# Edge messages of a graph network on one core: the gathered rows are added to the edge products in PSUM, and the gates stay in PSUM

## The reference, cut to what matters

```
edge_input = concatenate([x[src], edge_attr])                  # 200000 x (96 + 32)
messages = gelu(edge_input @ mW1 + mb1) @ mW2 + mb2
gates = sigmoid(gelu(edge_input @ gW1 + gb1) @ gW2 + gb2)      # one number for each edge
aggregated = segment_sum(messages * gates, dst)
```

## Time and profile before

| what | value |
|---|---|
| median of 3 executions | 5472.3 us (5466.99 to 5479.78) |
| the profiled execution's own time | 5465.93 us |
| span in its profile | 5464.0 us |
| busy: PE, DVE, ACT, POOL | 3652.2, 3789.0, 2527.0, 3536.7 us |
| gathers of line 790 for `rows` | 1568, 1791.1 us busy |
| they start between | 1519.8 and 3842.4 us |

### The profile page before, as it was taken

One profiled execution on the slowest core, in us unless ns is written; L12 is line 12 of the kernel. 1 busy time (PEld: TensorE's weight loads), 2 busy tenths in 40 slices (PEclk: granted clock), 3 DMA queues, 4 the chain that ended last, 5 costly groups with the idle time before them and its releaser, 6 DMA issues.

```text
span 5464.0 us, 92238 instructions
## 1 busy us (share of the span) xinstructions
PE 3652.2 (67%) x33772; PEld 2286.6 (42%) x33772; DVE 3789.0 (69%) x5678; ACT 2527.0 (46%) x4379; POOL 3536.7 (65%) x2920
## 2 busy tenths in 40 slices
PE   4899899999953333333333333333279999999999
PEld 3888899899931111111111111111233333333333
DVE  7999432544455665665665655655379999999999
ACT  5999110101023233233333233332158888888887
POOL 3699100000057777777777777777448888888888
PEclk9999999999966666666666666666589999999999
DMA  3344889698733333333333333333111212222121
GB/s 70 165 200 191 331 340 394 256 398 336 292 90 115 117 114 115 118 110 117 117 110 119 117 111 117 117 111 118 46 35 57 64 57 60 60 58 64 57 63 38
DMA packets 296561, 760.10 MB, mean 139 GB/s; under 512 B 81161, under 2 KB 183753, under 8 KB 289993
## 3 DMA queue, kind: packets, MB, share of 16 engines
q1 hardware_dynamic: 217496, 595.47, 29.4%
q0 software_dynamic: 78768, 160.85, 11.2%
HBM read 589.77 MB, written 166.38 MB: 138 GB/s over the span
## 4 chain that ended last, share of the span: by engine, by line
PE 41%; POOL 34%; issue 15%; DVE 6%; ACT 1%; another core or an unknown queue 1%; DVEq 1%; DMA 0%; ACTq 0%; POOLq 0%; SPq 0%
POOL GA L790 32%; PE p_e L1167 14%; PE p_tr L1307 10%; PE p_e L1292 9%; PE p_mm L1269 3%; PE p_mm L1098 1%; POOL VA L790 1%; DVE VA L2423 1%; PE p_tr L1026 1%; DVE VA L1965 1%; POOL VA L902 1%; PE p_tr L1085 1%; DVE VA L1963 1%; PE p_e L1244 0%
## 5 line engine op out<-in xcount | busy, mean ns | idle before, releaser
L790 POOL DMA_INDIRECT GA<-table_mg,VA x1568 | 1791.1, 1142 | 1487.9 <-DMA table_mg<-VA 955.4
L2423 DVE TENSOR_TENSOR VA<-VA,p_mm 128x1024 f32<-128x1024 f32 (+1 forms) x1204 | 1362.0, 1203 | 7.5 <-POOL VA L902 6.6
L902 POOL TENSOR_SCALAR VA<-VA 128x1024 f32<-128x1024 f32 (+1 forms) x1204 | 1236.2, 1046 | 168.8 <-ACT VA L1644 157.0
L1198 PE MATMUL p_e<-BD,EA 128*128 128x384 f32 x784 | 407.1, 671 | 731.9 <-DMA EA<-in_edge_t 731.3
L1644 ACT ACTIVATE VA<-p_e 128x1024 f32<-128x1024 f32 x602 | 615.8, 1023 | 178.6 <-PE p_e L1292 177.5
L1307 PE MATMUL p_tr<-VA,GA 128*32 128x512 f32 (+1 forms) x5096 | 641.8, 580 | 2.7 <-ACT GA L1664 2.1
L2235 DVE TENSOR_TENSOR GA<-GA 128x1344 f32<-128x1344 f32 x168 | 254.2, 1554 | 542.7 <-DMA GA<-table_mg,VA 530.1
L2263 DVE SCALAR_TENSOR_TENSOR R<-R,keep,M 128x97 f32<-128x97 f32 x1568 | 505.8, 323 | 124.8 <-issue 8.2
L1198 PEld LDWEIGHTS p_e<-BD,EA 128*128 128x128 f32 x784 | 205.0, 270 | 916.9 <-DMA EA<-in_edge_t 765.1
L1198 PE MATMUL p_tr<-BD,EA 128*128 128x384 f32 x392 | 210.8, 669 | 370.9 <-DMA EA<-in_edge_t 370.9
L1198 PE MATMUL p_mm<-BD,EA 128*128 128x384 f32 x392 | 207.4, 660 | 374.0 <-DMA EA<-in_edge_t 374.0
(11 more groups left out here) (267 smaller groups left out, 6616.6 us busy)
## 6 DMA issues: line engine op xcount, KB each, us to landing
GA<-adj SPq DMA_DIRECT2D x98, 800.0 KB, 6.1
VA<-adj SPq DMA_DIRECT2D x98, 800.0 KB, 6.1
run_m<-R SPq DMA_DIRECT2D x112, 700.0 KB, 3.9
GA<-adj SPq DMA_DIRECT2D x98, 768.0 KB, 6.1
VA<-adj SPq DMA_DIRECT2D x98, 768.0 KB, 6.1
H<-adj SPq DMA_DIRECT2D x56, 896.0 KB, 5.1
adj<-GA SPq DMA_DIRECT2D x25, 1568.0 KB, 5.3
adj<-VA SPq DMA_DIRECT2D x24, 1568.0 KB, 5.3
```

The source lines that it names most:

```text
L790: pool.indirect_dma_start(out=to, out_offset=None, in_=of, in_offset=bass.IndirectOffsetOnAxis(ap=at, axis=0)).then_inc(s, 16)
L902: pool.tensor_scalar(e, e, HIGH, LOW, ALU.min, ALU.max).then_inc(clipped, 1)
L1198: pe.matmul(p_h[m % len(p_h)][0:CH, 0:4 * D], EA[:, n % 2, k // 2, :], BD[:, 2 * (k % 2):2 * (k % 2) + 2, :, :].rearrange("p a b f -> p (a ...
L2423: dve.tensor_tensor(e, e, p_mm[n % 2][:, 0:cols_of(n)].unsqueeze(1).to_broadcast([P, 2, cols_of(n)]), ALU.mult).then_inc(weighed, 1)
```

## The change

ScalarE no longer copies the edge products to SBUF. VectorE reads them in PSUM as one input of the addition, takes the gathered rows as the other, and writes to `hid` in SBUF. The 28 halves of 96 columns of a batch are packed five to a PSUM bank (480 columns), so that a batch has 6 packs (`PACKS`) in place of 7 banks. A pack that crosses the border of a group of `EA` (768 columns) is made by two matmuls. `p_h` has seven banks; the eighth, `p_mm[1]`, holds `gate_row` (copied there once) and `gates`, which ScalarE's tanh now writes there. `hid` has two slots in place of four. TensorE waits on `rows_added`, since it is VectorE that frees a bank now.

```diff
-AHEAD_E = 2
-SLOTS_E = 4
+SLOTS_E = 2
+PACK = 5
+PACKS = -(-2 * U // PACK)
+ADDS = PACKS
...
-        p_h = [*p_e, *p_tr, *p_mm]
+        p_h = [*p_e, *p_tr, p_mm[0]]
...
-        gate_row = gw2[0:CH, :]
-        gates = small[:, 1, 0:U]
+        gate_row = p_mm[1][0:CH, 0:D]
+        gates = p_mm[1][0:CH, D:D + U]
...
+        def pack_halves(b):
+
+            return range(PACK * b, min(PACK * b + PACK, 2 * U))
...
                     if k >= 2:
-                        sp.wait_ge(edge_product, BANKS * (k - 1))
+                        sp.wait_ge(edge_product, PACKS * (k - 1))
...
-                    wait(pool, rows_added, 2 * (k - 1))
+                    wait(pool, rows_added, ADDS * (k - 1))
...
-                for m in range(BANKS * BATCHES):
-                    n, k = m // BANKS, m % BANKS
-                    if k == 0:
+                for m in range(PACKS * BATCHES):
+                    n, b = m // PACKS, m % PACKS
+                    if b == 0:
                         pe.wait_ge(edge_landed[n % 2], 16 * (n // 2 + 1))
-                    wait(pe, edges_kept, m - len(p_h) + 1)
-                    pe.matmul(p_h[m % len(p_h)][0:CH, 0:4 * D], EA[:, n % 2, k // 2, :],
-                              BD[:, 2 * (k % 2):2 * (k % 2) + 2, :, :].rearrange("p a b f -> p (a b f)"),
-                              start=True, stop=True).then_inc(edge_product, 1)
+                    wait(pe, rows_added, m - len(p_h) + 1)
+                    at_col = 0
+                    for g in range(UG):
+                        part = [v for v in pack_halves(b) if v // (2 * EG) == g]
+                        if not part:
+                            continue
+                        cols = slice(D * (part[0] - 2 * EG * g), D * (part[-1] + 1 - 2 * EG * g))
+                        mm = pe.matmul(p_h[m % len(p_h)][0:CH, at_col:at_col + D * len(part)], EA[:, n % 2, g, :],
+                                       BD[:, :, :, :].rearrange("p a b f -> p (a b f)")[:, cols], start=True, stop=True)
+                        at_col += D * len(part)
+                    mm.then_inc(edge_product, 1)
...
-                def keep_edges(n):
-
-                    wait(act, sums_ready[n % 2], (n - SLOTS_E) // 2 + 1)
-                    for k in range(BANKS):
-                        m = BANKS * n + k
-                        act.wait_ge(edge_product, m + 1)
-                        act.activation(hid[n % SLOTS_E][:, 2 * k:2 * k + 2, :],
-                                       p_h[m % len(p_h)][0:CH, 0:4 * D].rearrange("p (a f) -> p a f", a=2), ACT.Copy
-                                       ).then_inc(edges_kept, 1)
...
+                dve.tensor_copy(gate_row, gw2[0:CH, :])
...
-                    dve.wait_ge(edges_kept, BANKS * (n + 1))
                     dve.wait_ge(rows_landed[n % 2], 16 * U * (n // 2 + 1))
-                    for c in (0, 1):
-                        half = hid[n % SLOTS_E][:, BANKS * c:BANKS * (c + 1), :]
-                        dve.tensor_tensor(half, half, rows[:, n % 2, BANKS * c:BANKS * (c + 1), :], ALU.add
+                    of = rows[:, n % 2, :, :].rearrange("p u f -> p (u f)")
+                    for b in range(PACKS):
+                        m = PACKS * n + b
+                        dve.wait_ge(edge_product, m + 1)
+                        dve.tensor_tensor(hid_at[n % SLOTS_E][:, pack_cols(b)],
+                                          p_h[m % len(p_h)][0:CH, 0:D * len(pack_halves(b))], of[:, pack_cols(b)], ALU.add
                                           ).then_inc(rows_added, 1)
```

More of the change, by code:

```diff
@@ L346, in build @@
         p_sums = p_tr[0]
-        gate_row = gw2[0:CH, :]
-        gates = small[:, 1, 0:U]
+        gate_row = p_mm[1][0:CH, 0:D]
+        gates = p_mm[1][0:CH, D:D + U]
         rows = GA[0:CH, 0:2 * U * 2 * D].rearrange("p (h u f) -> p h u f", h=2, u=U)
-        hid_at = [*[GA[0:CH, (2 + k) * U * 2 * D:(3 + k) * U * 2 * D] for k in range(SLOTS_E - 1)], VA[0:CH, 0:U * 2 * D]]
+        hid_at = [GA[0:CH, (2 + k) * U * 2 * D:(3 + k) * U * 2 * D] for k in range(SLOTS_E)]
         hid = [a.rearrange("p (u f) -> p u f", u=U) for a in hid_at]
-        assert (SLOTS_E + 1) * U * 2 * D <= GA.shape[1] and U * 2 * D <= TILES * D
+        assert (SLOTS_E + 2) * U * 2 * D <= GA.shape[1]
         half_bias = small[:, 2, 0:1]
@@ L525, in products, with pack_cols @@
             return sum(len(bank_tiles(g, n_w)) for g in range(groups))
+        def pack_halves(b):
+            return range(PACK * b, min(PACK * b + PACK, 2 * U))
+        def pack_cols(b):
+            return slice(D * pack_halves(b).start, D * pack_halves(b).stop)
         def acc_steps(a):
@@ L1191, in sum_pass @@
                 pe.wait_ge(product_used, at["mm"])
[L1193 to L1195 removed]
+                for m in range(PACKS * BATCHES):
+                    n, b = m // PACKS, m % PACKS
+                    if b == 0:
                         pe.wait_ge(edge_landed[n % 2], 16 * (n // 2 + 1))
[L1197 to L1201 removed]
+                    wait(pe, rows_added, m - len(p_h) + 1)
[9 more added lines that the diff above has]
+                    mm.then_inc(edge_product, 1)
+                pe.wait_ge(rows_added, PACKS * BATCHES)
                 update_nodes()
@@ L1572, in sum_pass @@
             def sum_pass():
-                def keep_edges(n):
-                    wait(act, sums_ready[n % 2], (n - SLOTS_E) // 2 + 1)
-                    for k in range(BANKS):
-                        m = BANKS * n + k
-                        act.wait_ge(edge_product, m + 1)
-                        act.activation(hid[n % SLOTS_E][:, 2 * k:2 * k + 2, :],
-                                       p_h[m % len(p_h)][0:CH, 0:4 * D].rearrange("p (a f) -> p a f", a=2), ACT.Copy
-                                       ).then_inc(edges_kept, 1)
-                act.wait_ge(table_stored, 16 * GROUPS * 2)
-                for n in range(AHEAD_E):
-                    keep_edges(n)
                 for n in range(BATCHES):
-                    for c in (0, 1):
-                        half = hid[n % SLOTS_E][:, BANKS * c:BANKS * (c + 1), :]
-                        act.wait_ge(rows_added, 2 * n + c + 1)
-                        act.activation(half, half, ACT.Gelu).then_inc(gelu_done, 1)
+                    for lo, hi in ((0, PACKS // 2), (PACKS // 2, PACKS)):
+                        some = hid_at[n % SLOTS_E][:, pack_cols(lo).start:pack_cols(hi - 1).stop]
+                        act.wait_ge(rows_added, PACKS * n + hi)
+                        act.activation(some, some, ACT.Gelu).then_inc(gelu_done, 1)
                     act.wait_ge(logit_ready, n + 1)
                     act.activation(gates, small[:, 0, 0:U], ACT.Tanh, bias=half_bias, scale=0.5).then_inc(gate_ready, 1)
-                    if n + AHEAD_E < BATCHES:
-                        keep_edges(n + AHEAD_E)
             def scatter_pass(n):
```

4 lines of the change are left out of this document (removed).

## The result

Three runs of the changed kernel took 5420.28 to 5426.13 us, median 5422.25, against 5472.3 before: a ratio of 0.9905, 95% interval 0.9889 to 0.992. So it is faster, but by 50 us, under 1%, and not by 331, and lies outside the range (5122 to 5185). The profiled execution took 5426.13 us with a span of 5424.2.

What follows compares the result with a forecast made beforehand. GpSimd's issue of 1568 gathers was taken as the bound; 332 us of port holds gained less 1 us lost gave 5472.3 - 331 = 5141 us, with an 8-in-10 range of 5122 to 5185 us.

Steps and rivals of the forecast that it cites:

- Point 1: VectorE's additions and two multiplications lose one SBUF input and stop holding GpSimd's gathers: 332 us gained.
- Rivals A and B: A: port not freed in all three places, 5240 to 5260, both 5360 us (7%); B: nothing gained, 5472 us (4%).
- Point 2: VectorE's turn per batch grows by 0.3 to 14.2 us, still waiting some 3.3 us within 17.5 us of gathers.
- Point 4: TensorE's nine matmuls a batch take some 10 us, covered with 7.5 us to spare; uncovered, up to 10 us per batch.
- rival C: Slower: products come late at TensorE's waits on `rows_added`, turns of 24.2 us, 414 us more, 5890 us (2%).
- Rival D: Transfers cannot follow the gathers' faster pace: loss of perhaps 20 to 50 us, 5160 to 5190 us (3%).
- Point 5: Gathers wait for `rows_added` of batch k - 2: no wait but the first, once (29.8 us, some 0.5 more).
- the sum itself: Gather stage: 1567 steps of 0.949 + 0.302 us make 1960 us, with 29.8 us of waiting 1990, against 2322.6.
- the 29.8 us of the sum: GpSimd's one wait at the start of the gather stage, counted in the 1990 us.
- The holds: Long VectorE instructions with two SBUF inputs lengthen gathers beside them: mean 1142 ns against median 949, 303 us busy time.
- the gather's 0.94 us beside the addition: Sign for point 1: the gather at 3899.56 keeps its usual 0.94 us amid a 0.56 us addition from PSUM.
- the "odd 33 us" of point 1: Idle time of the gathers beyond 470 us, read as some 17 late starts at 1.91 us each, some rounding included.

Runs made afterwards that it cites:

- the third chip: Chip of the third follow-up group: kernel before 5406.1 us; changed kernel with one memset per gather 5099.58, two memsets 5100.19, a drain behind each 14 gathers 5368.63.
- groups one, two, four and five: Follow-up groups, each on another chip; the kernel before took 5474.7 us (first), 5480.3 (second), 5475.4 (fourth) and 5473.7 (fifth).

## Why the prediction was wrong

**What was right.** Point 1, the port: additions and multiplications with one input in PSUM don't hold gathers, in any of the three places and in either order of inputs (maximum 1046 ns). This is what the Trainium skill, page "SBUF — State Buffer", section "Who interferes with whom", says of VectorE instructions with at most one SBUF input, and the trace agrees. Rivals A and B are out. Point 2, VectorE's own work in a turn: 14.2 us forecast, 14.07 measured with the gathers left out. (1344 columns in 1.5 us are 0.90 columns per ns, and not the 0.96 of point 2 unless a fixed part is taken off first. The six additions took the 3.3 us all the same, from 2985.42 to 2988.69.) Point 4: with the gathers left out TensorE keeps up with turns of 14.07 us, and in the changed kernel no addition waited for a product that was still being made, so rival C is out. Rival D is out as well: the additions waited 2.1 us for rows in the whole stage. Point 5 held only where there are no stalls; in the changed kernel gathers waited 286.6 us for rows to be freed. And the sum itself came out on the third chip: the gathers start within 1993.2 us, where I had 1990:

```profile
L798 POOL DMA_INDIRECT GA<-table_mg,VA x1568: 940/946/4881, 1521.9 to 3515.1; - x196
...
L2240 DVE TENSOR_TENSOR GA<-p_e,GA x384: 446/648/659, 1554.1 to 3518.8; 128x480 f32<-128x480 f32 x160, 128x288 f32<-128x288 f32 x32
...
  DMA GA<-table_mg,VA: 389.7, 111
```

These are the rows of the kernel with one memset ahead of each gather, whose turn is the changed kernel's in all but that. VectorE's additions wait there for rows alone, 389.7 us in 111 turns or 3.5 us in each, where I had written "some 3.3 us"; they never wait for TensorE. The ratio was 0.9426, against a forecast of 5141 / 5472.3 = 0.9395. The changed kernel itself was not run on such a chip, so that it would take the same there is not shown.

**The step that failed.** Point 2 says "a batch of 14 gathers at 1.25 us will take 17.5 us, so VectorE still waits some 3.3 us in each turn", and rival D "gathers between the held ones already go at that pace". Both take for granted that the pace of one engine leaves the others' work as long as it was: that VectorE's turn stays 14.2 us beside gathers at 1.25 us, and that it is VectorE that waits. Measured were turns of 19.96 us, with GpSimd waiting for VectorE. On five of seven occasions (the first result and the chips of groups one, two, four and five) gathers that come at 1.25 us for longer than some 21 in a row make instructions of VectorE come late, and of ScalarE too, above all where it has copies to make (run sums mostly 1.40 us apart, at times 0.72, in place of 0.39), until GpSimd pauses. TensorE was not late. Gathers between the held ones go at 1.25 us, but never many of them.

The size. The stage was to last 1990 us and lasted 2264.4. Of the 274 us between them, 257 are what GpSimd waited for VectorE beyond the 29.8 us of the sum (286.6 in all); the rest are late starts. The holds had been (1142 - 949) ns x 14 = 2.7 us a batch, the drain that clears the stalls costs 2.7, and GpSimd's waiting is 2.56 a batch, so all three come out at 20 to 20.4 us. Why they lie so near to each other no run shows; it may be chance. It is not that the gathers' mean pace decides: with one wait for six products they were 1.48 us apart on average and with `gate_row` and `gates` alone 1.50, more than the 1.46 of the kernel before, and the stalls stayed. What the kernel before has instead is breaks: the holds themselves, and only 11 of its run sums come late. With `gate_row` and `gates` alone some 0.7 us of them are left in a batch, (998 - 949) ns x 14, and there are stalls. So I read the holds as no mere loss: on such a chip they did for the others what the drain does. The changed stage took 58.2 us less (2264.4 for 2322.6), began 12.6 us later, and what comes behind it took 5.8 us more: 39.8 us of span.

That taking away the two multiplications' holds alone was slower (ratio 1.0132) fits the same cause: less pause, and ScalarE's seven copies a batch left as work for the stalls to fall on. The full change takes those copies away, and this may be why it gains at all. It was not tested apart, and neither was the one bank fewer.

**The trace of before had shown it.** The 49 node gathers go at 1.25 us with nothing to hold them. While they last, ScalarE and VectorE stand:

```profile
3909.00 0.60 ACT L1539 ACTIVATE hT<-p_tr 97x512 f32<-97x512 f32 x1 [19.19 <-remote]
...
3920.20 0.59 ACT L1539 ACTIVATE hT<-p_tr 96x512 f32<-96x512 f32 x1 [10.60 <-remote]
...
3937.70 0.56 DVE L2279 TENSOR_TENSOR T<-p_mm,T 128x384 f32<-128x384 f32 x1 [37.11 <-remote]
```

I had quoted a row from this place, for the gather's 0.94 us beside the addition, and passed over the [9.95 <-remote] in the same line. That these waits are stalls and not the work's own order shows in the kernel with a memset ahead of each row gather on the third chip, where the node gathers have the same pace: from 11 us behind their start on no wait of VectorE is longer than 4.4 us and none of ScalarE longer than 2.6. The first 28 gathers are the other such place: they too run at 1.25 us, until 1555 us, and the waits around them are as long.

```profile
1549.46 0.56 DVE L2136 TENSOR_TENSOR T<-p_mm,B 128x384 f32<-128x384 f32 x1 [14.93 <-remote]
...
1557.14 0.59 ACT L1512 ACTIVATE hT<-p_tr 96x512 f32<-96x512 f32 x1 [19.07 <-remote]
```

On the third chip the stretch behind the last row gather is 5102.6 - 3515.1 = 1587.5 us long, against 5464.0 - 3842.4 = 1621.6 here. The kernel before was not profiled there, but the kernel with a drain behind 14 gathers was profiled on both kinds of chip, with the same turns: its spans are 5367.2 and 5440.2 us. Of the 73 us between them 35.7 lie behind the last row gather and 16.8 between the first and the last, most of it at the 29th, which starts 18.45 us behind the 28th on the chip with stalls and 3.95 on the other. The remaining 20.5 lie ahead of the first row gather, where runs on chips with stalls differ by up to 17 us among themselves; they are not explained. By this, most of the 61 to 74 us by which the kernel before differs between the chips would be such stalls at the node gathers and the first row gathers.

**What is open.** Why a chip has the stalls, and whether it is the chip or something of where or when the group ran; by which way a gather holds up other engines (its bytes don't matter, and neither does the bringing of VectorE's instructions); and how short a pause is enough, and how rare. Run sums came late only from the 22nd gather without a pause on, so one drain for 21 gathers in place of 14 might do; it was not tried. A version better than the change on a chip with stalls was not found.

## What to carry to other kernels

When an engine's holds are taken away, ask what the others do while it runs undisturbed, and look in the trace for a stretch where it already does: the waits in it that no engine explains ("issue", "remote") hint at the price. A gain worked out from one engine's pace needs the others' speed at that pace. And put the kernel before beside each run on the same chip: its own 5406 us in place of 5475 was the first sign that a cure was not one.

## What the runs showed of the hardware

- GpSimd's gathers (128 rows at once, 0.95 us each, 1.25 apart) made VectorE's and ScalarE's instructions late on five of seven occasions and not on two; TensorE was at most 0.1 us late in this stage. Without them the same work took 14.07 us a turn, with them 19.96 on average and up to 31 us in single turns.
- In every run without stalls at the first gathers it is a gather there that takes long: one or two of 3.6 to 5.8 us (maximum 4881 ns above), on the two chips without stalls, but also with eight memsets (5530 ns) or a memset and a drain (3594 ns) ahead of each gather on chips with stalls. In the runs with stalls there none takes more than 2.4 us.
- A GpSimd drain behind a gather put the next one off by 2.15 us (3.40 for 1.25, a memset included) or, once in 14, by 2.7; a single small memset or a fulfilled semaphore wait takes none of the 1.25 us.
- Every 112th row gather starts 1.9 us late (some 3.15 us behind the last in place of 1.25; with eight memsets 3.17 in place of 2.13), before and after the change and on both kinds of chip, with memsets between the gathers or without, unless GpSimd waits for rows just then. I had put part of these late starts down to the port (the "odd 33 us" of point 1).
